# Gated feed-forwards of a 16-layer kernel: each fp32 product as three float32r products of operands split on chip

## Chip, cores, metric

One Trainium2 chip, one core. The metric is the device time of one execution in microseconds; the kernel before takes 3042.12 us (median of three runs, 3042.0 to 3043.24).

## What is computed

A stack of 16 layers on 1024 tokens of width 256, all in fp32: attentions, scans, and feed-forwards, each with a normalisation ahead of it and its result added to x. Six of them go through the function that is changed. With h the normalised tokens:

```python
# gated feed-forward (twice; 8 tiles of 128 inner rows; the gate has a low-rank part added)
out = (silu(h @ W_in.T + low_rank) * (h @ W_up.T)) @ W_down.T
# experts (twice; 32 experts x 96 inner rows = 24 tiles)
w = renormalised top-8 of softmax(h @ router.T), cut at a share of 0.8
out = sum_e w[:, e] * ((silu(h @ gate_e.T) * (h @ up_e.T)) @ down_e.T)
# ternary (twice; 704 inner rows, padded to 6 tiles; one scale per inner row and per output column)
out = (silu(h @ gate.T * gate_s) * (h @ up.T * up_s)) @ down.T * down_s
```

## The kernel before, in words

All layers run on one core, each in a stage of its own with five instruction streams (SP for transfers, TensorE, ScalarE, VectorE, GpSimd) that meet by semaphores. x and the transposed normalised tokens hT (128 x 2 x 1024) stay in SBUF. The end of a stage already makes the next one's first products and holds its first two weight tiles.

`gated_feed_forward` (L2227) does all six. A tile is 128 inner rows: 512 columns of gate and up weights and 256 of down weights, side by side in one of RING buffers (6, or 7 for the experts). A unit u is half a tile's tokens: tile u//2, tokens 512(u%2) onward. TensorE's order is written out by hand (L2413 to L2436): `project_gate(u)` (L2349), `project_up(u)` (L2373), then `lower(u - LAG)` (L2395), the down product of a unit LAG steps back (LAG 8, experts 10). Gate and up are two 128x512 matmuls each into PSUM; down is four matmuls of 256 columns, whose stationary side is a 128-token piece of the inner tile. ScalarE makes the silu (L2465), VectorE multiplies it by the up product into one of INNER buffers (L2484, ternary L2480). For the experts GpSimd then multiplies by the routing weight (L2338), which SP has spread over partitions (L2305) from a small DRAM table (L2313); for the ternary layers it scales the down weights in place (L2332). VectorE's routing chain (`choose`, L2493) has the first seven multiplies placed in it by hand, and TensorE transposes the routing weights in unit 7 (L2423). SP refills a weight buffer when the down product of its tile is done (L2296).

After the last unit the down products of the last LAG units are closed output tile by output tile (L2437 to L2446); each is added to x (L183), its statistics taken, its normalised row made and transposed for the next stage. Where the next layer has the kind "norm", VectorE has more steps for it (L237 to L243, L326). The core of TensorE's loop:

```python
for u in range(0, UNITS, 2):
    project_gate(u)
    if low_rank is None:
        project_up(u)
        if u >= LAG:
            lower(u - LAG)
        project_gate(u + 1)
```

Of the kernel before, what the change touches and what calls it, by code (L numbers as in the profile page):

```python
# [6 lines left out]
ALU = mybir.AluOpType  # L7
# [4 lines left out]
U32 = mybir.dt.uint32  # L12

P = 128
TOK = 1024
# [2211 lines left out]
def gated_feed_forward(core, name, first_w, tiles, source=None, scaled=False, low_rank=None, router=None,  # L2227
# [6 lines left out]

# [3 lines left out]
    UNITS, INNER, SPREAD = 2 * tiles, LAG + 2, 3  # L2238
# [5 lines left out]
    with Stage(core, name) as st:  # L2244
        following = core.next.open(st)
        block = st.opened
        w = [*first_w, *[st.sb(f"w{n}", [P, wide]) for n in range(len(first_w), RING)]]
        gate = [st.sb(f"gate{n}", [P, HALF]) for n in range(2)]
        inner = [st.sb(f"inner{n}", [P, HALF]) for n in range(INNER)]
        if router is not None:  # L2250
# [22 lines left out]
        copied, stored, found = st.sem("copied"), st.sem("stored"), st.sem("found")  # L2273

# [13 lines left out]
        def wait_inner(engine, u):  # L2288

            engine.wait_ge(multiplied if router is None else weighted, u + 1)  # L2290
# [54 lines left out]
        def _(pe):  # L2345
            def tokens_of(u):
                return slice(u % 2 * HALF, (u % 2 + 1) * HALF)

            def project_gate(u):  # L2349
                n = u // 2  # L2350
# [4 lines left out]
                wait_weights(pe, n)  # L2355
                if u >= 2:
                    pe.wait_ge(silued, u - 1)
                for c in range(DC):
                    last = nc.tensor.matmul(ps_gate[u % 2][:], w[n % RING][:, c * P:(c + 1) * P],  # L2359
                                            hT[:, c, tokens_of(u)], start=(c == 0),  # L2360
                                            stop=(c == DC - 1 and low_rank is None))
# [3 lines left out]
            def add_low_rank(u):  # L2365

                for half in range(2):
# [5 lines left out]
            def project_up(u):  # L2373
                n = u // 2
# [5 lines left out]
                for c in range(DC):  # L2380
                    last = nc.tensor.matmul(ps_up[u % 2][:], w[n % RING][:, D + c * P:D + (c + 1) * P],  # L2381
                                            hT[:, c, tokens_of(u)], start=(c == 0), stop=(c == DC - 1))
                last.then_inc(upped, 1)

            def down(u, t):
                return nc.tensor.matmul(out_of(t), inner[u % INNER][:, t % 4 * P:(t % 4 + 1) * P],  # L2386
                                        w[u // 2 % RING][:, 2 * D:3 * D], start=(u == 0), stop=(u >= UNITS - 2),
# [1504 lines left out]
```

## Time and profile before

| | |
|---|---|
| median of three runs | 3042.12 us |
| profiled execution: span, first to last instruction | 3038.4 us |
| its own time | not listed beside the runs; they are 3.6 to 4.8 us over its span |
| busy: TensorE, VectorE, ScalarE, GpSimd | 96%, 44%, 39%, 19% |
| mean granted TensorE clock | 0.993 |
| data moved | 121.96 MB, mean 40 GB/s |

Times in the profile are from the span's start. PE is TensorE's matmuls, PEld its loads of the stationary operand, DVE VectorE, ACT ScalarE, POOL GpSimd, SPq the transfer queue. An fp32 matmul appears as two records. A record's duration includes the pipeline, so neighbours overlap; the pitch is read from starts. In a timeline row that merges x records, the time is from the first's start to the last's end.

### The profile page before, as it was taken

The numbers are of one execution on the slowest core, as the hardware profiler recorded it, in microseconds if no ns is written. First come the engines' busy times: TensorE is split into PE (matmuls) and PEld (weight loads), VectorE is DVE, ScalarE is ACT, GpSimd is POOL, SyncE is SP. The second block draws the span as 40 slices with busy tenths as digits, with TensorE's granted clock in tenths as the row PEclk, the third lists the DMA queues.
The fourth block names the chain that finished last, engine by engine and source line by source line (L and its number), as shares of the span: only waits on it lengthen the run. The fifth ranks groups of instructions, "written<-read, shape, count | busy, mean of one in ns | idle before, by whom it ended". The sixth has DMA issues, their size and how long they took to land. (4 is left out here: it accounts for less than half of the span.)

```text
span 3038.4 us, 40714 instructions
## 1 busy us (share of the span) xinstructions
PE 2909.8 (96%) x14953; PEld 1767.2 (58%) x14953; DVE 1351.2 (44%) x3173; ACT 1171.7 (39%) x2389; POOL 586.7 (19%) x737
## 2 busy tenths in 40 slices
PE   7989999999999999999999999999999999999979
PEld 4444455644475555556666666646676677754545
DVE  7758425686144114211333333333333332258588
ACT  4636514546132113111443333433334343236576
POOL 2030001130012222222000000012333332130086
PEclk9999999999999999999999999999999999999999
DMA  3021000020102331332100000000000010121021
GB/s 98 18 67 47 26 25 27 9 79 2 51 12 87 88 99 50 90 92 85 39 16 11 11 11 11 18 32 11 12 16 11 16 39 13 39 43 43 13 88 60
DMA packets 69361, 121.96 MB, mean 40 GB/s; under 512 B 15790, under 2 KB 44816, under 8 KB 68896
## 3 DMA queue, kind: packets, MB, share of 16 engines
q1 hardware_dynamic: 67564, 118.04, 13.1%
q8 instruction: 121, 1.98, 0.3%
q10 hardware_dynamic: 1600, 1.31, 0.3%
q14 instruction: 76, 0.62, 0.1%
HBM read 92.21 MB, written 1.54 MB: 31 GB/s over the span
## 5 line engine op out<-in xcount | busy, mean ns | idle before, releaser
L222 POOL TENSOR_TENSOR scale<-scale,powers 128x1 f32<-128x1 f32 (+1 forms) x98 | 57.4, 586 | 1396.9 <-DVE scale L203 1396.9
L2484 DVE TENSOR_TENSOR L1f_inner<-psum,L1f_gate 128x512 f32<-128x512 f32 x96 | 66.4, 691 | 350.7 <-PE psum L2381 350.6
L1688 ACT ACTIVATE L2b_tanh<-psum,L2b_inverse 128x512 f32<-128x512 f32 x192 | 110.6, 579 | 269.7 <-PE psum L1636 268.3
L2465 ACT ACTIVATE L1f_gate<-psum 128x512 f32<-128x512 f32 x96 | 57.1, 597 | 388.0 <-PE psum L2359 388.0
L1267 ACT ACTIVATE L0f_weights<-psum 128x512 f32<-128x512 f32 (+2 forms) x320 | 156.9, 567 | 93.1 <-PE psum L1083 72.1
L2338 POOL TENSOR_TENSOR L1f_inner<-L1f_inner,L1f_weight 128x512 f32<-128x512 f32 x96 | 119.2, 1265 | 354.5 <-DMA L1f_weight<-combine 339.0
L1645 PEld LDWEIGHTS psum<-L2b_v,L2b_weights 128*128 128x128 f32 x1152 | 139.6, 191 | 40.2 <-issue 28.7
L2125 ACT ACTIVATE L2a_probs<-psum,L2a_negmax 128x512 f32<-128x512 f32 (+7 forms) x128 | 95.0, 742 | 172.4 <-DVE L2a_negmax L2159 172.3
L1636 PE MATMUL psum<-L2b_q,L2b_k 128*128 128x512 f32 (+3 forms) x384 | 149.9, 487 | 1.0 <-DVE L2b_q L1754 0.8
L1645 PE MATMUL psum<-L2b_v,L2b_weights 128*128 128x129 f32 x1152 | 143.6, 276 | 5.8 <-POOL L2b_weights L1554 5.8
L2012 PE MATMUL psum<-L2a_k,L2a_q 128*128 128x512 f32 (+3 forms) x384 | 145.1, 487 | 0.0
L2159 DVE TENSOR_REDUCE L2a_negmax<-psum 128x1 f32<-128x512 f32 (+7 forms) x128 | 96.6, 755 | 81.6 <-PE psum L2014 81.5
L2169 DVE COPY L2a_probsT<-psum 128x512 f32<-128x512 f32 (+1 forms) x64 | 31.4, 491 | 227.9 <-PE psum L2025 227.9
L2043 PE MATMUL psum<-L2a_probsT,L2a_v 128*128 128x512 f32 (+3 forms) x384 | 129.4, 486 | 0.3 <-DVEq L2197 0.3
L2386 PE MATMUL psum<-L1f_w,L1f_inner 128*128 128x256 f32 x512 | 122.9, 379 | 0.0
L1049 PE MATMUL psum<-L0f_ks,L0f_qs 96*128 96x512 bf16 (+3 forms) x384 | 111.3, 331 | 9.9 <-DVE L0f_piece_max L1348 5.6
L1995 PE MATMUL psum<-hT,L2a_early 128*128 128x512 f32 x248 | 119.8, 606 | 0.7 <-PEq L102 0.7
L2381 PE MATMUL psum<-hT,L1f_w 128*128 128x512 f32 x256 | 120.3, 592 | 0.0
L2359 PE MATMUL psum<-hT,L1f_w 128*128 128x512 f32 x256 | 120.3, 592 | 0.0
L1619 PE MATMUL psum<-hT,L2b_early 128*128 128x512 f32 x248 | 116.5, 593 | 1.0 <-PEq L102 1.0
L2386 PEld LDWEIGHTS psum<-L1f_w,L1f_inner 128*128 128x128 f32 x512 | 96.7, 190 | 35.0 <-issue 22.3
L1080 PE MATMUL psum<-L0f_qs,L0f_ks 99*128 99x512 bf16 (+3 forms) x384 | 111.8, 328 | 3.8 <-ACT L0f_weights L1267 2.1
(537 smaller groups left out, 6152.7 us busy)
## 6 DMA issues: line engine op xcount, KB each, us to landing
L1f_w<-in_L1f_w SPq DMA_DIRECT2D x32, 384.0 KB, 3.8
L1f_weight<-combine SPq DMA_DIRECT2D x32, 384.0 KB, 4.4
L1f_weight<-combine SPq DMA_DIRECT2D x32, 256.0 KB, 4.8
scan_spread_b<-bc SPq DMA_DIRECT2D x16, 512.0 KB, 3.8
L0f_qs<-L0f_part SPq DMA_DIRECT2D x96, 64.0 KB, 2.6
experts_early<-in_L1f_w SPq DMA_DIRECT2D x16, 384.0 KB, 3.4
L2a_early<-in_L2a_w SPq DMA_DIRECT2D x16, 384.0 KB, 3.0
L2b_early<-in_L2b_w SPq DMA_DIRECT2D x16, 384.0 KB, 3.1
```

What stands on the lines that cost most here:

```text
L1080: last = nc.tensor.matmul(to, ks[:, kt // 4, h, kt % 4 * P:(kt % 4 + 1) * P], qs[:, half, h, at:], start=True, stop=not masks)
L1267: nc.scalar.activation(to, src, ACT.Exp, scale=HD ** -0.5).then_inc(exped, 1)
L1619: last = nc.tensor.matmul(to[:], w[e][:, c, at:at + P], hT[:, c, half * HALF:(half + 1) * HALF], start=(c == 0), stop=(c == DC - 1))
L1636: nc.tensor.matmul(ps_scores[u % 3][:, at:], k[e][:, kt * P:(kt + 1) * P], q[e][:, half * HALF + at:(half + 1) * HALF], start=True, stop=T ...
L1645: last = nc.tensor.matmul(ps_out[t % 2][:, 0:P + 1], weights[UNITS.index((kt, t // 4))][:, at:at + P], v[e][:, kt, :], start=(kt == 0), st ...
L1995: last = nc.tensor.matmul(to[:], w[h % 2][:, c, at:at + P], hT[:, c, half * HALF:(half + 1) * HALF], start=(c == 0), stop=(c == DC - 1))
L2012: nc.tensor.matmul(ps_scores[i % 2][:, a:b], q[h % 2][:, t * P:(t + 1) * P], k[h % 2][:, a:b], start=True, stop=b < width(i))
L2043: last = nc.tensor.matmul(to[:, at:], v[h % 2][:, kt, :], probsT[h % 2][half][:, kt, at:], start=(kt == 0), stop=(kt == tiles - 1))
L2338: nc.gpsimd.tensor_tensor(inner[u % INNER][:], inner[u % INNER][:], weight[n % SPREAD][:, half * HALF:(half + 1) * HALF], ALU.mult).then_i ...
L2359: last = nc.tensor.matmul(ps_gate[u % 2][:], w[n % RING][:, c * P:(c + 1) * P], hT[:, c, tokens_of(u)], start=(c == 0), stop=(c == DC - 1 ...
L2381: last = nc.tensor.matmul(ps_up[u % 2][:], w[n % RING][:, D + c * P:D + (c + 1) * P], hT[:, c, tokens_of(u)], start=(c == 0), stop=(c == D ...
L2386: return nc.tensor.matmul(out_of(t), inner[u % INNER][:, t % 4 * P:(t % 4 + 1) * P], w[u // 2 % RING][:, 2 * D:3 * D], start=(u == 0), sto ...
```

## The change

Every operand of the three products is split on chip into a high part, a copy written as float32r, and its rest, the difference written as float32r. A product a.b becomes high.high + high.rest + rest.high, three matmuls into the same PSUM tile (`products`, `multiply_parts`). ScalarE makes the high parts, VectorE the rests. The gate and up products of the first WHOLE = 1 tile stay fp32; all down products are split. The tokens are split once per layer (four copies, four subtractions), the gate and up weights of a tile two tiles ahead, the down weights by `down_of_step`, the inner tile BEHIND steps after its multiply (1, experts 8). A weight buffer is now refilled when its down weights have been split. In the routing chain the token split and the steps' subtractions stand between the old steps. An excerpt of the diff:

```diff
+def products(stationary, moving):
+    return [(stationary[0], moving[0]), (stationary[0], moving[1]), (stationary[1], moving[0])]
+def multiply_parts(nc, to, pairs, start, stop, skip=False):
+    for n, (stationary, moving) in enumerate(pairs):
+        last = nc.tensor.matmul(to, stationary, moving, start=start and n == 0, stop=stop and n == len(pairs) - 1,
+                                skip_group_check=skip)
+    return last
...
-    UNITS, INNER, SPREAD = 2 * tiles, LAG + 2, 3
+    UNITS, WHOLE, WIDE_PARTS, DOWN_PARTS, SPREAD = 2 * tiles, 1, 3, LAG // 2 + 1, 3
+    BEHIND = 1 if router is None else LAG - 2
+    INNER = BEHIND + 2
...
+        def wide_of_step(s):
+            n = s // 2 + WHOLE + 1
+            return n if s % 2 == 0 and n < tiles else None
+        def down_of_step(s):
+            m = (s - LAG + 3) // 2
+            return m if s % 2 and 0 <= m < tiles else None
+        STEPS_IN_ALL = max(UNITS + BEHIND, 2 * tiles + LAG - 3)
...
-                    sp.wait_ge(lowered, 2 * (n - RING) + 2)
+                    sp.wait_ge(down_low, n - RING + 1)
...
+            def project(u, to, at, open_ended=False):
...
+                pe.wait_ge(hT_low, DC * 2)
+                pe.wait_ge(wide_low, n - WHOLE + 1)
+                pairs = []
+                for c in range(DC):
+                    pairs += products([part[:, at + c * P:at + (c + 1) * P] for part in wide_parts[n % WIDE_PARTS]],
+                                      [part[:, c, tokens_of(u)] for part in hT_parts])
+                return multiply_parts(nc, to, pairs, start=True, stop=not open_ended)
...
             def wait_down(u):
-                wait_inner(pe, u)
-                if down_by is not None:
-                    pe.wait_ge(down_scaled, u // 2 + 1)
+                pe.wait_ge(inner_low, u + 1)
+                pe.wait_ge(down_low, u // 2 + 1)
...
+            def high_wide(n):
+                wait_weights(act, n)
+                if n >= WHOLE + WIDE_PARTS:
+                    act.wait_ge(upped, 2 * (n - WIDE_PARTS) + 2)
+                nc.scalar.copy(wide_parts[n % WIDE_PARTS][0][:], w[n % RING][:, 0:2 * D]).then_inc(wide_high, 1)
...
+            def high_inner(u):
+                act.wait_ge(multiplied if router is None else weighted, u + 1)
+                if u >= LAG:
+                    act.wait_ge(lowered, u - LAG + 1)
+                nc.scalar.copy(inner_parts[u % LAG][0][:], inner[u % INNER][:]).then_inc(inner_high, 1)
...
+            for half in range(2):
+                for c in range(DC):
+                    high_tokens(c, half)
+            high_wide(WHOLE)
             if router is not None:
                 act.wait_ge(shifted, 1)
                 nc.scalar.activation(p[:], logits[:], ACT.Exp).then_inc(exped, 1)
-            for u in range(UNITS):
+            for s in range(STEPS_IN_ALL):
+                if s < UNITS:
+                    find_gate(s)
+                if wide_of_step(s) is not None:
+                    high_wide(wide_of_step(s))
+                if down_of_step(s) is not None:
+                    high_down(down_of_step(s))
+                if BEHIND <= s < UNITS + BEHIND:
+                    high_inner(s - BEHIND)
...
+            def low_inner(u):
+                dve.wait_ge(inner_high, u + 1)
+                high, low = inner_parts[u % LAG]
+                nc.vector.tensor_tensor(low[:], inner[u % INNER][:], high[:], ALU.subtract).then_inc(inner_low, 1)
...
                 nc.vector.tensor_tensor(logits[:], ps_logits, over_experts(peak), ALU.subtract).then_inc(shifted, 1)
+                low_tokens()
                 dve.wait_ge(exped, 1)
...
                 multiply(0)
+                after_multiply(0)
```

`high_down`, `low_wide`, `low_down` and `high_tokens` are of the same form; `low_tokens` ends with `low_wide(WHOLE)`, and `after_multiply(s)` makes VectorE's wide, down and inner rests of step s in that order.

## Rows read from the trace of the kernel before

**Rows 1.** The page's first part: busy time and share of the span by engine.
```profile
PE 2909.8 (96%) x14953; PEld 1767.2 (58%) x14953; DVE 1351.2 (44%) x3173; ACT 1171.7 (39%) x2389; POOL 586.7 (19%) x737
```

**Rows 2.** Timeline in mid-layer: start us, us, engine, line, operation, operands, count.
```profile
1102.49 1.88 PE L2359 MATMUL psum<-hT,L1f_w 128*128 128x512 f32 x4
...
1104.20 1.88 PE L2381 MATMUL psum<-hT,L1f_w 128*128 128x512 f32 x4
...
1105.92 1.89 PE L2386 MATMUL psum<-experts_early,L1f_inner 128*128 128x256 f32 x8
...
1107.65 1.88 PE L2359 MATMUL psum<-hT,L1f_w 128*128 128x512 f32 x4
```

**Rows 3.** Window of the first expert layer: stretch, length, busy by engine, clock, DMA.
```profile
922.45:1175.50 253.05, 253.00 (x821) 151.01 (x822) 58.99 (x147) 37.82 (x65) 65.81 (x63) 1.00 0.30 86
```

**Rows 4.** Groups by line and shape: busy us, mean ns of one, idle before.
```profile
L332 PE MATMUL psum<-zeros 128*128 128x512 bf16 x109 | 28.0, 393 | 0.0
...
L2025 PE MATMUL psum<-ident,L2a_probs 128*128 128x128 f32 x576 | 84.3, 273 | 6.7 <-ACT L2a_probsT L2133 4.9
...
L1645 PEld LDWEIGHTS psum<-L2b_v,L2b_weights 128*128 128x128 f32 x1152 | 139.6, 191 | 40.2 <-issue 28.7 <-POOL L2b_weights L1554 11.5
```

**Rows 5.** Timeline: bf16 matmuls; transposes; fp32 loads and matmuls of 129 columns.
```profile
1180.94 3.62 PE L332 MATMUL psum<-zeros 128*128 128x512 bf16 x16
...
1907.36 0.71 PE L2025 MATMUL psum<-ident,L2a_probs 128*128 128x128 f32 x5
...
2199.53 0.86 PEld L1645 LDWEIGHTS psum<-L2b_v,L2b_weights 128*128 128x128 f32 x7 [0.24 <-issue]
...
2199.75 0.83 PE L1645 MATMUL psum<-L2b_v,L2b_weights 128*128 128x129 f32 x6
```

**Rows 6.** Groups as in rows 4: ScalarE, VectorE and GpSimd.
```profile
L1695 ACT ACTIVATE L2b_weights<-L2b_tanh 128x512 f32<-128x512 f32 x96 | 59.5, 620 | 0.0
...
L1695 ACT ACTIVATE L2b_weights<-L2b_tanh 128x256 f32<-128x256 f32 x32 | 13.2, 413 | 0.0
...
L2484 DVE TENSOR_TENSOR L1f_inner<-psum,L1f_gate 128x512 f32<-128x512 f32 x96 | 66.4, 691 | 350.7 <-PE psum L2381 350.6
...
L3121 DVE TENSOR_TENSOR scan_fed<-scan_delta,hT 128x512 f32<-128x512 f32 x4 | 5.6, 1400 | 0.1
...
L2338 POOL TENSOR_TENSOR L1f_inner<-L1f_inner,L1f_weight 128x512 f32<-128x512 f32 x96 | 119.2, 1265 | 354.5 <-DMA L1f_weight<-combine 339.0 <-DVE L1f_inner L2484 15.5
```

**Rows 7.** Start of the first expert layer: one window, then the timeline.
```profile
926.26:945.70 19.44, 19.44 (x46) 8.51 (x46) 18.16 (x70) 5.56 (x9) 0.00 (x0) 1.00 0.14 57
...
948.55 1.04 PE L2423 MATMUL psum<-ident,L1f_weights 128*32 128x128 f32 x8
...
957.26 12.28 POOL L2338 TENSOR_TENSOR L1f_inner<-L1f_inner,L1f_weight 128x512 f32<-128x512 f32 x10 [38.99 <-DMA L1f_weight<-combine]
...
961.44 1.89 PE L2386 MATMUL psum<-experts_early,L1f_inner 128*128 128x256 f32 x8
```

**Rows 8.** Timeline, start of the first ternary layer.
```profile
2023.68 0.69 ACT L2465 ACTIVATE L2f_gate<-psum,L2f_early 128x512 f32<-128x512 f32 x1
...
2026.27 1.88 PE L2359 MATMUL psum<-hT,L2f_early 128*128 128x512 f32 x4
```

**Rows 9.** Timeline, end of the first expert layer.
```profile
1150.64 1.88 PE L2381 MATMUL psum<-hT,L1f_w 128*128 128x512 f32 x4
...
1156.45 0.42 DVE L183 TENSOR_TENSOR x<-x,psum 128x256 f32<-128x256 f32 x1 [3.14 <-PE psum L2386]
```

**Rows 10.** Timeline, end of the first gated layer, VectorE.
```profile
446.87 0.42 DVE L183 TENSOR_TENSOR x<-x,psum 128x256 f32<-128x256 f32 x1
...
448.82 0.42 DVE L183 TENSOR_TENSOR x<-x,psum 128x256 f32<-128x256 f32 x1 [0.20 <-PE psum L2386]
```

**Rows 11.** Windows behind that end, columns as in rows 3.
```profile
454.00:458.00 4.00, 0.84 (x5) 0.48 (x4) 3.69 (x17) 1.08 (x2) 1.96 (x4) 1.00 0.00 0
...
460.00:462.00 2.00, 2.00 (x5) 1.00 (x4) 0.59 (x3) 0.00 (x0) 0.00 (x0) 0.50 0.00 0
```

More of the change, by code:

```diff
@@ L12 @@
 U32 = mybir.dt.uint32
+F32R = mybir.dt.float32r
 P = 128
@@ L2247, in gated_feed_forward @@
         w = [*first_w, *[st.sb(f"w{n}", [P, wide]) for n in range(len(first_w), RING)]]
+        hT_parts = [st.sb(f"hT_part{i}", [P, DC, TOK], F32R) for i in range(2)]
+        wide_parts = [[st.sb(f"wide{n}_{i}", [P, 2 * D], F32R) for i in range(2)] for n in range(WIDE_PARTS)]
+        down_parts = [[st.sb(f"down{n}_{i}", [P, D], F32R) for i in range(2)] for n in range(DOWN_PARTS)]
         gate = [st.sb(f"gate{n}", [P, HALF]) for n in range(2)]
         inner = [st.sb(f"inner{n}", [P, HALF]) for n in range(INNER)]
+        inner_parts = [[st.sb(f"inner_part{n}_{i}", [P, HALF], F32R) for i in range(2)] for n in range(LAG)]
         if router is not None:
@@ L2354, in project_gate @@
                     return
-                wait_weights(pe, n)
                 if u >= 2:
                     pe.wait_ge(silued, u - 1)
[L2358 to L2361, printed above, removed]
+                last = project(u, ps_gate[u % 2][:], 0, open_ended=low_rank is not None)
                 if low_rank is None:
@@ L2379, in project_up @@
                     pe.wait_ge(multiplied, u - 1)
[L2380 to L2383, printed above, removed]
+                project(u, ps_up[u % 2][:], D).then_inc(upped, 1)
             def down(u, t):
-                return nc.tensor.matmul(out_of(t), inner[u % INNER][:, t % 4 * P:(t % 4 + 1) * P],
-                                        w[u // 2 % RING][:, 2 * D:3 * D], start=(u == 0), stop=(u >= UNITS - 2),
-                                        skip_group_check=True)
+                at = t % 4 * P
+                return multiply_parts(nc, out_of(t),
+                                      products([part[:, at:at + P] for part in inner_parts[u % LAG]],
+                                               [part[:] for part in down_parts[u // 2 % DOWN_PARTS]]),
+                                      start=u == 0, stop=u >= UNITS - 2, skip=True)
             def wait_down(u):
-                wait_inner(pe, u)
-                if down_by is not None:
-                    pe.wait_ge(down_scaled, u // 2 + 1)
+                pe.wait_ge(inner_low, u + 1)
+                pe.wait_ge(down_low, u // 2 + 1)
             def lower(u):
@@ L2456, in _, with find_gate @@
         def _(act):
-            if router is not None:
-                act.wait_ge(shifted, 1)
-                nc.scalar.activation(p[:], logits[:], ACT.Exp).then_inc(exped, 1)
-            for u in range(UNITS):
+            def find_gate(u):
                 act.wait_ge(gated, u + 1)
@@ L2527, in choose @@
                 multiply(2)
+                after_multiply(2)
                 for t in range(NT):
@@ L2542, in choose @@
                 multiply(5)
+                after_multiply(5)
                 multiply(6)
+                after_multiply(6)
                 for n in range(2):
@@ L2547, in choose, with low_tokens @@
                                           ).then_inc(copied, 1)
-            if router is not None:
+            def low_tokens():
+                for half in range(2):
+                    for c in range(DC):
+                        part = slice(half * HALF, (half + 1) * HALF)
+                        dve.wait_ge(hT_high, DC * half + c + 1)
+                        nc.vector.tensor_tensor(hT_parts[1][:, c, part], hT[:, c, part], hT_parts[0][:, c, part],
+                                                ALU.subtract).then_inc(hT_low, 1)
+                low_wide(WHOLE)
+            if router is None:
+                low_tokens()
+            else:
                 choose()
-            for u in range(0 if router is None else 7, UNITS):
-                multiply(u)
+            for s in range(0 if router is None else 7, STEPS_IN_ALL):
+                if s < UNITS:
+                    multiply(s)
+                after_multiply(s)
             for t in range(NT):
```

48 lines of the change are left out of this document (43 added, 5 removed).

## The prediction

> **What bounds the kernel now.** I read the page's first part first: TensorE is busy for 96% of the span, every other engine for less than half [rows 1]. Busy time of pipelined multiplies overstates work, so the next view is the timeline of one stretch in the middle of an expert feed-forward, where the starts of the groups give the true pitch. There the gate product starts at 1102.49, the up product at 1104.20, the down products at 1105.92 and the next unit's gate at 1107.65 [rows 2]. So a unit (half a tile: 128 inner rows x 512 tokens) costs 5.16 us: 3.43 for two products of two 128x512 fp32 matmuls each (0.86 us a matmul, two records of 0.43) and 1.72 for four 128x256 matmuls (0.43 each, two records of 0.215). TensorE starts each piece when the one before lets it go. The windows of a whole expert layer show the same: 253.00 of 253.05 us busy, VectorE 59, ScalarE 38, GpSimd 66, clock 1.00 [rows 3]. The bound is TensorE's column passes: four passes of a product's columns at 0.215 us per 512, in two records.
>
> The six gated layers have 16+16+48+48+12+12 = 152 units, so 152 x 5.16 = 784 us of the run is what the change touches.
>
> **What the change removes and adds on TensorE.** An fp32 matmul becomes three float32r ones. No row of this kernel runs that type. Lower bound of its price: the rate of a 2-byte operand, one column pass. The 16 bf16 128x512 matmuls, each with a load of its own, end 3.62 us after the first starts; less the last one's own 0.39 that is 15 pitches of 0.215 us [rows 4, 5]. Upper bound: one fp32 record, 0.43 us per 512 columns [rows 2]; the nearest row of a single 4-byte record, the transposes of 128 columns, speaks for it: 5 of them in 0.71 us, each 0.27 long, so (0.71 - 0.27)/4 = 0.11 us per 128 columns, twice the bf16 rate [rows 4, 5]. I take 0.215: an fp32 product here is exactly four passes of one column each, which is what two halves of one operand times two halves of the other would be, and a type made for operands cut to a high part has no reason to split again; the transposes move exact bits in 128-column pieces and need not be the same path. It stays the main uncertainty.
>
> The load of the stationary tile counts too, once per pass: in the down products a pass of 256 columns is only 0.107 us. The nearest rows are the 128x129 fp32 records with their loads: 7 loads of 0.19 in 0.86 us, (0.86 - 0.19)/6 = 0.112 us apart, beside 6 matmuls in 0.83, with the transposes' 0.27 for the last one (0.83 - 0.27)/5 = 0.11 apart [rows 4, 5]. A load per 0.112 us is hidden, so a down pass costs 0.111. The other bound is a load in the open at its full 0.19.
> - Gate and up: tile 0 stays fp32, so 140 units x 4 matmuls = 560, each 0.86 - 3 x 0.215 = 0.215 less: 120.4 us.
> - Down: all 152 units x 4 = 608, each 0.43 - 0.333 = 0.097 less: 59.0 us.
> - Sum 179.4 us. The unit becomes 2.58 + 1.33 = 3.91 us.
>
> A rule of the Trainium skill speaks against this. First the row: loads of 0.19 us follow each other at 0.112 us while matmuls on the same 128 rows run at 0.11 [rows 5], so they lie under them. The skill (TensorE: Matmul & The Clock Gate, What overlaps and what doesn't) says that a weight load overlaps running matmuls only when it goes to another row group; by that rule each of the new passes would show its load. The trace contradicts it, so I give it a small chance only; its price is a rival below.
>
> **The splitting work, beside TensorE.** Per unit ScalarE gets one 128x512 copy of the inner tile, and per tile one of 128x512 and one of 128x256. By its row of an SBUF source (620 and 413 ns) that is 0.62 + (0.62 + 0.41)/2 = 1.14 us on top of a 0.6 us silu. VectorE gets subtractions: 0.69 + (0.69 + 0.42)/2 = 1.25 us on top of its 0.69 multiply [rows 6, 10]. Both stay under 2 us in a 3.91 us unit. Each part is made ahead of use: wide parts four units, inner parts at least two, so these chains cost nothing while that lead holds. In the expert layers GpSimd's multiply (1.265 us a unit) reads the same memory; one 128x512 VectorE product of two SBUF tiles took 1.40 us where 0.69 is usual, which I read as such a clash [rows 6]. Even doubled, 2.5 + 0.69 = 3.2 us is below 3.91. Transfers: a weight tile's load now waits for the low part of the down weights, four units earlier than it waited for the down product; SP's queue is not longer and the order of the spread weights is unchanged. Cost 0.
>
> **The edges, where that lead does not exist.**
> - Start of an expert layer. VectorE runs the routing chain 18.16 us busy in the 19.44 up to 945.70, when the weights are reduced; TensorE asks for them only at 948.55, and the first down product starts at 961.44 [rows 7]. Now VectorE gets, inside that chain, four token subtractions and four to five wide ones (9 x 0.69 = 6.2, of which 0.5 fills a wait for ScalarE), so the routing weights come at 951.4; TensorE, now faster, waits for them. From the transposes to GpSimd's first product took 957.26 - 948.55 = 8.7 us (copies, a store, the spread) [rows 7]; with two multiplies and a subtraction now ahead of the copies 10.2, so GpSimd starts at 961.7. Its product, the copy, the subtraction (1.27 + 0.62 + 0.69) and handovers put the first down product at 964.6. Unhindered it would be at 961.44 - 9 x 0.86 = 953.7. Loss 10.9 us a layer, 22 in two.
> - Start of the other four. In a ternary layer silu used to start at 2023.68, behind its table load [rows 8]; it now stands behind five copies (3 us), and the gate product of unit 2, at 2026.27, waits for it: to 2027.4. Loss 1.2 each, 5 in all. The first layer's tokens are copied while the fp32 tile 0 runs, so that cover is nearly whole.
> - End of an expert layer. The low parts run 8 units behind the multiply, so after the last multiply VectorE still has 8 inner and 3 down subtractions and one more: about 8 us, with ScalarE beside it. Up to now four down matmuls were followed at once by the closing sums (last up product 1150.64, first sum 1156.45) [rows 9]. TensorE needs unit 46's part for its first closing sum and gets it 8 us after the last up product, having 2.9 us of work: loss 5.5 each, 11.
> - End of the other four: one unit behind, but three down parts late: 1.2 each, 5.
> - The first layer's end is followed by a norm with more VectorE steps: its sums already come 1.95 us apart (446.87, 448.82) against 1.72 of TensorE [rows 10], so the 8 x 0.4 us saved there is lost: 3.
> - Clock. After 3.2 us without work in 454 to 458 the granted clock was 0.50 in 460 to 462 [rows 11], which is the lower level. The new hole at the expert layers' ends may do it: 2.5 each, 5.
>
> Sum of the edges 51. Net 179 - 51 = **128 us less**. The rows are of one execution with a span of 3038.4 us; its own time is not listed, but the three runs (median 3042.12) are 3.7 us over the span, so I take that for what lies around it. 3042.1 - 128 = **2914 us**. Its own range: edges of 25 to 80 us and a down pass of 0.107 to 0.12 give 2885 to 2950.
>
> **Rivals.**
> - Slower: a float32r pass costs what one fp32 record costs. Place: every pass of the gated layers. Gate and up then cost 1.29 for 0.86 (+0.43 x 560 = +241), down 0.645 for 0.43 (+0.215 x 608 = +131); the edges half as much (+25): **3440 us**. For it: the transposes' 0.11 us. Against it: bf16's 0.215 [rows 5]. It decides from the pass price at which 560(0.86 - 3p) + 608(0.43 - 1.5p) = 51, p = 0.27 us per 512 columns. A compiler that turns these matmuls into the two-record form would be the same rival in a worse size. 0.11.
> - Loads in the open everywhere: 1680 + 1824 = 3504 passes x 0.111 = +389: **3303 us**. This is what the skill's rule would do here. Against it: the hidden loads [rows 5]. 0.03.
> - Only the down passes limited by loads of 0.19: 608 x (0.57 - 0.333) = +144: **3058 us**. 0.04, half of it so near no change that I count 0.02 there.
> - VectorE and GpSimd hold each other up in the expert layers, the unit going to 4.6 us rather than 3.91: 96 x 0.7 = +67: **2981 us**. For it: the doubled subtraction [rows 6]. 0.08.
> - The forecast: 0.74.
>
> **Numbers.** 0.2% (6 us) is about what a measurement of this kernel can tell from no change. Faster is forecast and the fourth rival: 0.82; same 0.02; slower 0.16. The range that holds 8 in 10 takes the forecast's own and the fourth rival: 2875 to 2990.
>
> **What would show it.** The new matmul records: single, 512 columns 0.215 us apart and 256 columns 0.107 to 0.112. A unit in mid-layer 3.9 us long, with no wait of TensorE for a low part. TensorE idle before the first down product of an expert layer and before its closing sums, nowhere else over 2 us. Passes 0.43 us apart, or a unit over 5.16 us, would prove the forecast wrong; so would VectorE busy without gaps in mid-layer.

## The result and the profile after

The changed kernel takes 2953.52 us (median of four runs, 2952.19 to 2954.47) beside 3042.06 us (four runs, 3040.25 to 3043.24) for the kernel before: a ratio of 0.9709, 95% interval 0.9695 to 0.9723. That is 88.5 us less, where the forecast was 128 less, so 39 us above the forecast. It lies inside the range given for 8 cases in 10 (2875 to 2990) and 3.5 us outside the forecast's own (2885 to 2950).

The first part of the profile's page, after:

```profile
span 2952.7 us, 44166 instructions
...
PE 2796.7 (95%) x16121; PEld 1871.8 (63%) x16121; DVE 1606.9 (54%) x3495; ACT 1324.7 (45%) x2711; POOL 613.0 (21%) x737
```

TensorE lost 113 us of busy time against [rows 1], VectorE gained 256 and ScalarE 153, and TensorE is still the bound. Groups by line (busy us, mean ns of one, then idle before):

```profile
L130 PE MATMUL psum<-L1f_hT_part,L1f_wide 128*128 128x512 f32 x1104 | 271.7, 396 | 6.1 <-DVE L1f_inner L2561 5.5
...
L2369 POOL TENSOR_TENSOR L1f_inner<-L1f_inner,L1f_weight 128x512 f32<-128x512 f32 x96 | 143.1, 1500 | 268.0 <-DVE L1f_inner L2561 177.6
L130 PE MATMUL psum<-L1f_down,L1f_inner_part 128*128 128x256 f32 x1152 | 159.7, 291 | 16.1 <-DVE L1f_inner_part L2577 16.1
...
L2577 DVE TENSOR_TENSOR L1f_inner_part<-L1f_inner,L1f_inner_part 128x512 fp32r<-128x512 f32 x96 | 142.3, 1491 | 10.5 <-ACT L1f_inner_part L2521 10.5
```

The float32r products are one record each (1104 is 92 units of two products of six; the labels say f32). TensorE has two new waits of some size: that for the inner tiles' rests, 16.1 us in 12 waits, and that for VectorE's multiply (L2561), 5.5 us in 9 waits, all of them at the layers' edges. Timeline of TensorE in mid-layer, to be held against [rows 2]:

```profile
1040.63 2.91 PE L130 MATMUL psum<-L1f_hT_part,L1f_wide 128*128 128x512 f32 x12
1043.37 1.59 PE L130 MATMUL psum<-L1f_down,L1f_inner_part 128*128 128x256 f32 x12
1044.81 2.91 PE L130 MATMUL psum<-L1f_hT_part,L1f_wide 128*128 128x512 f32 x12
```

Group starts give the pitch: 2.74 us for twelve gate and up passes, 1.44 for twelve down passes, no wait between them. The unit is 4.18 us; it was 5.16, and 3.91 was forecast. From start to start of single records a 512-column pass is 0.227 us and a 256-column pass 0.120.

Start of the first expert layer, TensorE (own products begin at 902.85), then its end:

```profile
902.85 5.38 PE L130 MATMUL psum<-hT,experts_early 128*128 128x512 f32 x8
...
926.86 1.03 PE L2461 MATMUL psum<-ident,L1f_weights 128*32 128x128 f32 x8
927.65 9.81 PE L130 MATMUL psum<-L1f_hT_part,L1f_wide 128*128 128x512 f32 x42
939.82 1.91 PE L130 MATMUL psum<-L1f_down,L1f_inner_part 128*128 128x256 f32 x12 [2.35 <-DVE L1f_inner_part L2577]
941.52 4.31 PE L130 MATMUL psum<-L1f_hT_part,L1f_wide 128*128 128x512 f32 x12
...
1097.71 1.95 PE L130 MATMUL psum<-L1f_down,L1f_inner_part 128*128 128x256 f32 x15
1101.34 0.63 PE L130 MATMUL psum<-L1f_down,L1f_inner_part 128*128 128x256 f32 x3 [1.68 <-DVE L1f_inner_part L2577]
1102.88 0.63 PE L130 MATMUL psum<-L1f_down,L1f_inner_part 128*128 128x256 f32 x3 [0.91 <-DVE L1f_inner_part L2577]
1104.42 0.62 PE L130 MATMUL psum<-L1f_down,L1f_inner_part 128*128 128x256 f32 x3 [0.91 <-DVE L1f_inner_part L2577]
1105.96 8.56 PE L130 MATMUL psum<-L1f_down,L1f_inner_part 128*128 128x256 f32 x48 [0.92 <-DVE L1f_inner_part L2577]
```

The hole ahead of the first down product and the one ahead of the closing sums are where the prediction put them, 2.35 and 4.4 us (1.68 + 0.91 + 0.91 + 0.92), and behind each TensorE runs slower. Windows (columns as in [rows 3], the last three numbers being clock, DMA share and GB/s):

```profile
940.00:945.00 5.00, 5.00 (x22) 4.23 (x23) 3.48 (x4) 0.45 (x1) 5.00 (x4) 0.66 0.59 184
1104.00:1112.00 8.00, 6.66 (x32) 6.46 (x33) 4.87 (x13) 0.60 (x1) 1.24 (x3) 0.57 0.01 2
```

A granted clock of 0.66 and 0.57 of 2.4 GHz means that most of each stretch ran at 1.2 GHz.

Where the time went, by stage (from a stage's first TensorE product to the next stage's first, one profiled execution each):

| stage | before | after | saved in passes at 0.227 and 0.120 | given back at the edges |
|---|---|---|---|---|
| gated, two layers | 100.6, 94.0 | 89.8, 81.2 | 14.6, 14.6 | 3.8, 1.8 |
| experts, two layers | 254.9, 255.0 | 228.3, 228.4 | 46.5, 46.5 | 19.9, 19.9 |
| ternary, two layers | 64.9, 64.3 | 56.7, 56.5 | 10.6, 10.6 | 2.4, 2.8 |
| all other stages, to TensorE's last product | 2201 | 2208 | 0 | 7 |

The fourth column: an fp32 product of 512 columns for three passes saves 0.86 - 0.68 = 0.18 us, one of 256 columns 0.43 - 0.36 = 0.07, so an expert layer saves 184 x 0.18 + 192 x 0.07 = 46.5. These prices are rounded. By the unit, which fell by 5.16 - 4.18 = 0.98 us where all of it is split and by 1.72 - 1.44 = 0.28 where only the down products are, an expert layer saves 46 x 0.98 + 2 x 0.28 = 45.6, and its edges give back 19.0.

### The profile page after: what moved, and what is told of

Read it like the earlier page. It is cut to its first block and busy times, and to the rows that moved or that the text cites. A ratio compares the mean times of both kernels' runs of the same rounds, so it can differ in the third digit from the quotient of the medians.

```text
span 2952.7 us, 44166 instructions
## 1 busy us (share of the span) xinstructions
PE 2796.7 (95%) x16121; PEld 1871.8 (63%) x16121; DVE 1606.9 (54%) x3495; ACT 1324.7 (45%) x2711; POOL 613.0 (21%) x737
## 3 DMA queue, kind: packets, MB, share of 16 engines
q10 hardware_dynamic: 1600, 1.31, 0.3%
## 5 line engine op out<-in xcount | busy, mean ns | idle before, releaser
L130 PE MATMUL psum<-L1f_hT_part,L1f_wide 128*128 128x512 f32 x1104 | 271.7, 396 | 6.1 <-DVE L1f_inner L2561 5.5
L130 PEld LDWEIGHTS psum<-L1f_hT_part,L1f_wide 128*128 128x128 f32 x1104 | 203.8, 190 | 50.8 <-DVE L1f_inner L2561 9.6
L2369 POOL TENSOR_TENSOR L1f_inner<-L1f_inner,L1f_weight 128x512 f32<-128x512 f32 x96 | 143.1, 1500 | 268.0 <-DVE L1f_inner L2561 177.6
L130 PE MATMUL psum<-L1f_down,L1f_inner_part 128*128 128x256 f32 x1152 | 159.7, 291 | 16.1 <-DVE L1f_inner_part L2577 16.1
L130 PEld LDWEIGHTS psum<-L1f_down,L1f_inner_part 128*128 128x128 f32 x1152 | 154.1, 198 | 25.0 <-DVE L1f_inner_part L2577 19.4
L2577 DVE TENSOR_TENSOR L1f_inner_part<-L1f_inner,L1f_inner_part 128x512 fp32r<-128x512 f32 x96 | 142.3, 1491 | 10.5 <-ACT L1f_inner_part L2521 10.5
L2147 ACT COPY L2a_probsT<-psum 128x512 f32<-128x512 f32 (+3 forms) x128 | 64.7, 505 | 124.1 <-PE psum L2039 122.3
L2561 DVE TENSOR_TENSOR L1f_inner<-psum,L1f_gate 128x512 f32<-128x512 f32 x96 | 66.0, 689 | 97.6 <-ACT L1f_gate L2500 94.0
```

The lines of the kernel that those rows point to most:

```text
L130: last = nc.tensor.matmul(to, stationary, moving, start=start and n == 0, stop=stop and n == len(pairs) - 1, skip_group_check=skip)
L2369: nc.gpsimd.tensor_tensor(inner[u % INNER][:], inner[u % INNER][:], weight[n % SPREAD][:, half * HALF:(half + 1) * HALF], ALU.mult).then_i ...
L2577: nc.vector.tensor_tensor(low[:], inner[u % INNER][:], high[:], ALU.subtract).then_inc(inner_low, 1)
```

## The experiments

The theory after the result: the mechanism is the one forecast (fewer column passes on TensorE, with the splitting hidden in mid-layer), and the miss is the price of a float32r pass, 12 and 9 ns over the forecast on each of 3504 passes. Rivals: the loads of the stationary tiles set the pitch; the edges or the split work cost more than they seem to. They come in the order of the argument.

**1. The price of a pass by itself.** In the changed kernel, a later stage first does 219 matmuls of no use to the result, in groups (2986.09 us in its single run):

```diff
+            group(r_wide, r_token, 20, 512)
+            group(r_wide, r_token, 20, 384)
...
+            group(r_wide, r_token, 20, 128)
+            group(r_wide, r_token, 19, 512, turn=True)
+            group(r_wide, r_token, 20, 480, m=32)
+            group(r_wide, r_token, 20, 240, m=32)
+            group(b_wide, b_token, 20, 512)
...
```

> One look. The decay stage gets extra matmuls whose results are dropped, on real data: float32r with a 128-column load of its own and 512, 384, 256, 192 and 128 columns, one group that changes its stationary tile each time, two groups that load only 32 columns (480 and 240 moving), and bf16 with 512, 256 and 128 columns. Theory A (a float32r pass has a fixed price of its own beside one column per 2.4 GHz cycle): pitches N/2.4 + 13 ns, so about 227, 173, 120, 93 ns, the same with a changing stationary tile, and still 213 and 113 ns with the 32-column load; bf16 without it: 215, 109. Theory B (the 13 ns are the 128-column 4-byte load that does not quite hide): with the 32-column load the pitch falls to 202 and 102 ns. At 128 columns the load may set the pitch (112 ns or more) under both.

Measured, the median time from one record's start to the next one's, in ns:

| columns | 512 | 384 | 256 | 192 | 128 | 480, 32 wide | 240, 32 wide |
|---|---|---|---|---|---|---|---|
| float32r | 227 | 173 | 120 | 111 | 111 | 213 | 107 |
| bf16 | 216 | | 109 | | 56 | | |

The weight loads of these groups (count, then the duration of one as min/median/max in ns, first and last start, forms):

```profile
L2833 PEld LDWEIGHTS psum<-decay_r_token,decay_r_wide x159: 107/188/193, 1135.7 to 1161.4; 128*128 128x128 f32 x119, 128*32 128x32 f32 x40
...
L2833 PEld LDWEIGHTS psum<-decay_b_token,decay_b_wide x60: 96/98/99, 1161.6 to 1169.1; 128*128 128x128 bf16 x60
```

At 2.4 GHz a column takes 0.417 ns, so 512, 384 and 256 columns are 213, 160 and 107 ns, and the pass is 13 ns more at each: a fixed part, not a rate. bf16 pays 2 to 3 ns. Below 256 columns another limit takes over: 111 ns, for 192 and for 128 columns alike, with a 4-byte 128x128 tile loaded before each, while a 2-byte tile allows 56. With a stationary tile of 32 columns, 240 moving columns go at 107, which is under that floor. So 111 is no floor of every 4-byte pass; it fits the 128-column load, and the down passes at 120 stay above it. Whether the 32-column load, itself 107 to 108 ns long, sets a floor at 107 was not run. The fixed 13 ns holds with one stationary address repeated and with two in turn (227 each). It does not hold at 240 columns with 32 wide, where 7 are left; that stays open. Nor does it hold at the lower clock: in the half-clock stretches of the changed kernel (942 to 945 and 1106 to 1111) the starts are 426 or 427 ns apart for 512 columns and 213 or 214 for 256, which is the columns at 1.2 GHz and nothing more.

The loads are 188 ns long and follow each other at 111 to 120 in the groups of 256 columns and fewer. So they lie under the matmuls on the same rows, as [rows 5] had said. The rule of the Trainium skill (TensorE: Matmul & The Clock Gate, What overlaps and what doesn't), that a load overlaps only matmuls of another row group, is not what these runs show.

**2. The parts in bfloat16.** This kernel rounds both parts to bfloat16, so the rest loses bits too and some 16 bits of each operand are kept, which is less than the change keeps (no run measured the error):

```diff
-        hT_parts = [st.sb(f"hT_part{i}", [P, DC, TOK], F32R) for i in range(2)]
+        hT_parts = [st.sb(f"hT_part{i}", [P, DC, TOK], BF16) for i in range(2)]
...
```

> All parts are stored as bf16 in place of float32r; everything else, the three passes, waits and order, stays. The rest is then rounded to 8 bits, so the third part of each operand's precision is left out. If the missing 39 us of the forecast are the float32r pass price (227 and 120 ns in place of 215 and 111), the passes go back to about 215 and 109 ns, 1680 x 0.012 + 1824 x 0.011 = 40 us less than the changed kernel: about 2914 us. If they come from the three-pass pattern, its loads or its waits, the time stays at about 2953.

2917.74 us (2917.41 to 2919.85), ratio 0.9597 (0.958 to 0.9613), 36 us less than the changed kernel. Mid-layer timeline of TensorE:

```profile
1043.21 2.75 PE L130 MATMUL psum<-L1f_hT_part,L1f_wide 128*128 128x512 bf16 x12
1045.80 1.47 PE L130 MATMUL psum<-L1f_down,L1f_inner_part 128*128 128x256 bf16 x12
1047.11 2.75 PE L130 MATMUL psum<-L1f_hT_part,L1f_wide 128*128 128x512 bf16 x12
```

The unit is 3.90 us, where 3.91 was forecast for float32r, and the time is 4 us from the forecast's 2914. Where the passes cost what the prediction had put for them (2.59 and 1.31 us for twelve), its sum comes out within 4 us; so the price was what was wrong.

**3 and 4. One half of the change at a time.** The down product back in fp32, with the old wait before a weight buffer's refill, and in another kernel gate and up back in fp32:

```diff
-                    sp.wait_ge(down_low, n - RING + 1)
+                    sp.wait_ge(lowered, 2 * (n - RING) + 2)
...
-                return multiply_parts(nc, out_of(t), ...
+                return nc.tensor.matmul(out_of(t), inner[u % INNER][:, at:at + P], w[u // 2 % RING][:, 2 * D:3 * D],
```

> Only gate and up products are split; the down products are fp32 again, with their old waits. By the pass price, 608 x (0.43 - 0.36) = 43 us are given back; the edges at the layers' ends (about 4.4 us of waits and some 3 us of half clock in each expert layer, 1.2 in the other four) go: 2953 + 43 - 20 = about 2976 us. The rival, that the down split hurts more than it brings because its edges and VectorE's extra work weigh more, says 2953 or less.

> Only the down products are split; gate and up are fp32 as before. By the pass price 560 x (0.86 - 0.68) = 101 us are given back, and the starts lose their waits (some 8 us in each expert layer, 1 to 2 in the others): 2953 + 101 - 22 = about 3032 us. With e3 this says whether the two savings add up: 43 + 101 of passes.

Down in fp32: 2998.4 us (2993.75 to 3005.49), ratio 0.9857 (0.9841 to 0.9874), 22 us over the expectation. Gate and up in fp32: 3025.6 us (3020.97 to 3026.68), 0.9947 (0.993 to 0.9963), within 7 us of it. The first shows a side of the change that the prediction had priced at nothing. ScalarE in mid-layer, timeline:

```profile
990.04 0.62 ACT L2505 CAST L1f_wide<-L1f_w 128x512 fp32r<-128x512 f32 x1 [7.46 <-DMA L1f_w<-in_L1f_w]
...
999.93 0.62 ACT L2505 CAST L1f_wide<-L1f_w 128x512 fp32r<-128x512 f32 x1 [8.29 <-DMA L1f_w<-in_L1f_w]
```

ScalarE waits for the weights themselves, and TensorE for the silu queued behind that copy (12.7 us in four waits in the gated layers, 7.5 in 19 in the expert layers). Gate and up weights are now needed two tiles ahead, but the buffer is refilled only once its down product is done. In the changed kernel the down weights are copied out early, so the refill starts early.

**5. The down product in fp32 with two more weight buffers** (the rings 8 and 9 instead of 6 and 7, else as the third):

```diff
-    LAG, RING = (8, 6) if router is None else (10, 7)
+    LAG, RING = (8, 8) if router is None else (10, 9)
```

> The second product in fp32 again, as in the run that took 2998.4 us, with two more weight buffers in the ring, so that a buffer's refill can start two expert pairs earlier. Theory A (what that run lost above its 2976 us was the refill, which goes back to waiting for the last product): 2972 to 2985 us, and the waits of ScalarE's weight rounding on the weight DMA go. Theory B (the fp32 product itself costs more than its share): 2993 to 3003 us.

2967.4 us (2965.94 to 2971.2), ratio 0.9763 (0.9748 to 0.9778): below both theories. ScalarE's waits for the weights are gone, and 31 us of the third kernel's loss were the late refill. What is left is that splitting the down product, 42.6 us of saved passes, is worth 14 us (2967.4 - 2953.4, the mean of the changed kernel's two medians). The stages say where. The four other layers take 294.9 us for 284.2, so there it pays 10.7. The expert layers take 228.4 and 229.3 us: practically what the changed kernel takes. Its timeline around the two edges:

```profile
934.61 9.81 PE L130 MATMUL psum<-L1f_hT_part,L1f_wide 128*128 128x512 f32 x42
944.45 1.99 PE L2424 MATMUL psum<-experts_early,L1f_inner 128*128 128x256 f32 x8
...
1106.68 3.08 PE L130 MATMUL psum<-L1f_hT_part,L1f_wide 128*128 128x512 f32 x12
1109.61 2.32 PE L2424 MATMUL psum<-experts_early,L1f_inner 128*128 128x256 f32 x10
1111.76 1.89 PE L2424 MATMUL psum<-L1f_w,L1f_inner 128*128 128x256 f32 x8
```

Neither hole is there and the clock stays at 1.00. Its 184 gate and up products save 33.1 us, so an expert layer gives back 228.4 - (254.9 - 33.1) = 6.6 us at its edges instead of 19.9. So 13.3 of the 19.9 come from the inner tiles' split, and that is what 192 down products save (13.4). In the expert layers half of the change earns nothing. (The changed kernel was not run with the larger ring; it has no wait for weights in mid-layer that the ring could remove.)

**6. Two passes instead of three.** This kernel leaves out rest.high, a third of the products' work:

```diff
-    return [(stationary[0], moving[0]), (stationary[0], moving[1]), (stationary[1], moving[0])]
+    return [(stationary[0], moving[0]), (stationary[0], moving[1])]
```

> The third product (rest times high) is left out, nothing else. TensorE's work falls by a third: 560 x 0.227 + 608 x 0.12 = 200 us, to a unit of 2.78 us, about 2755 us if the splitting stays hidden. If VectorE, which in the changed kernel needs 0.69 + 1.49 + 0.55 us a unit in the expert layers beside GpSimd's 1.5, is nearly the next bound there, the expert unit stays at 3.2 us or more and the time at 2790 or above. This measures how much cover is left.

2788.34 us (2787.04 to 2788.87), ratio 0.9168 (0.9154 to 0.9182). The run asks how near VectorE is to being the bound, and neither expectation came true as a whole. TensorE's waits for the inner tiles' rests grew from 16.1 to 26.9 us and those for VectorE's multiply from 5.5 to 13.8, all at the edges. Mid-layer timeline of TensorE:

```profile
1010.07 2.00 PE L130 MATMUL psum<-L1f_hT_part,L1f_wide 128*128 128x512 f32 x8
1011.91 1.12 PE L130 MATMUL psum<-L1f_down,L1f_inner_part 128*128 128x256 f32 x8
1012.86 2.00 PE L130 MATMUL psum<-L1f_hT_part,L1f_wide 128*128 128x512 f32 x8
```

The unit is 2.79 us, two thirds of 4.18, and mid-layer TensorE works without a wait. But a window of 80 us there has VectorE (the third number) without a gap too:

```profile
930.00:1010.00 80.00, 80.00 (x461) 70.45 (x460) 80.00 (x87) 43.64 (x86) 43.65 (x29) 1.00 0.59 167
```

At 2.79 us a unit the two engines tie, so the total comes out near what the theory of a VectorE bound had said, though through the edges: an expert layer has 48 units x 1.39 = 67 us of passes less and got 51 us shorter (228.3 to 177.3). The changed kernel at 4.18 us is well clear of that limit, and with VectorE's work as it is nothing below 2.8 us a unit could be had from TensorE alone (an inference from this tie, not a run).

**7 to 9. The edges.** The seventh kernel splits inner tiles three steps behind instead of eight once the routing is over, the eighth gives the token and first weight rests of the expert layers to GpSimd, which is idle there, and the ninth does both:

```diff
+        lag = BEHIND if router is None or s < 20 else 3
...
+                        nc.gpsimd.tensor_tensor(hT_parts[1][:, c, part], hT[:, c, part], hT_parts[0][:, c, part],
+                                                ALU.subtract).then_inc(hT_low, 1)
```

> In the expert layers the split of the inner tile, 8 steps behind the multiply, catches up from step 20 on by two tiles a step until it is 3 behind. Theory (the hole before the closing sums is VectorE's backlog): the 4.4 us of waits there shrink to 1 or 2 and the half clock behind it may go too: 3 to 6 us less a layer, 2941 to 2947 us. Rival (TensorE waits there for the last multiply and GpSimd's product in any case): no change, 2953.

> In the expert layers the rests of the tokens and of the first four split weight tiles are made by GpSimd, which is idle there, and leave VectorE's routing chain. Theory (the start is bound by that chain): the routing weights come some 5 us earlier, the first down product 4 to 5 us earlier, and the 2.35 us hole with its half clock may shrink: 8 to 12 us less in two layers, 2941 to 2945. Rival (GpSimd and VectorE hold each other up on shared memory access, and the spread of the routing weights sets the start): within 3 us of 2953.

> e6 and e7 together. If the two holes are separate, their gains add: 2930 to 2938 us.

2947.37 us (2945.3 to 2951.78; 0.9695, 0.9682 to 0.9708), 2950.27 (2947.73 to 2953.86; 0.9705, 0.9691 to 0.9718) and 2946.03 (2943.51 to 2947.35; 0.9689, 0.9675 to 0.9702). The intervals overlap that of the changed kernel, so a gain of 3 to 7 us is likely and none is certain. The seventh is 0.4 us over the upper end of its expectation, the eighth as the rival there had it, and the ninth missed. With the early split the end's hole is 2.7 us instead of 4.4:

```profile
1102.12 0.59 PE L130 MATMUL psum<-L1f_down,L1f_inner_part 128*128 128x256 f32 x3 [1.75 <-DVE L1f_down L2578]
1103.66 6.34 PE L130 MATMUL psum<-L1f_down,L1f_inner_part 128*128 128x256 f32 x51 [0.95 <-DVE L1f_down L2578]
```

In this execution of the seventh kernel those 51 passes run at full clock behind a hole of 2.7 us; at the end of the second expert layer, behind the same hole, some of them are at half clock.

The start has to be counted from each layer's own first TensorE product (896.49 with GpSimd's help, 899.28 without). With that help VectorE has eight subtractions less ahead of its sum of the routing weights, 4.8 us at a pitch of 0.6, yet that sum begins only 1.3 us sooner (23.9 for 25.2), and so do GpSimd's first weighted product (36.1 for 37.4) and the first down product (39.2 for 40.5). Both holes stay, 1.79 and 1.99 us for 2.35 and 1.28. GpSimd's timeline:

```profile
932.61 2.51 POOL L2380 TENSOR_TENSOR L1f_inner<-L1f_inner,L1f_weight 128x512 f32<-128x512 f32 x2 [17.00 <-DMA L1f_weight<-combine]
936.08 10.62 POOL L2380 TENSOR_TENSOR L1f_inner<-L1f_inner,L1f_weight 128x512 f32<-128x512 f32 x8 [0.96 <-DMA L1f_weight<-combine]
```

So what VectorE's chain gains is passed on in full, but it gains little. The trace says where the rest of the 4.8 us went. Three of VectorE's routing steps ran beside a GpSimd subtraction and took 0.94, 1.15 and 1.51 us for 0.42, 0.18 and 0.42, which is 2.6 us; 0.5 is a wait for ScalarE's exponential, and the chain's first step came 0.4 later. So the two engines do hold each other up, as the rival of this run had it. Behind the chain stands the path from the transposes over the spread of the weights to GpSimd's first product: 9.3 us here, 9.9 in the changed kernel, where 10.2 was forecast.

**10. The changed kernel once more**, to see what repeats:

> The changed kernel with no edit, beside the variants of this group. If the 7 us that the untouched layers lost and the granted clock of 0.984 belong to the change, they are there again: 2950 to 2956 us, untouched stages at 2208 us, clock 0.984. If they were an accident of one profiled execution, this profile shows untouched stages near 2201 us, at a clock above 0.986.

2953.25 us (2951.76 to 2958.27), ratio 0.9717 (0.9702 to 0.9731). The untouched stages took 2206 us at a mean clock of 0.987, between the two expectations. Over all the variants they took 2202 to 2210, against 2201 in the one profile of before. A part of the 7 us is one execution's: 2.8 of them lie in one attention stage (170.5 us before, 173.3 after), which took 170.3 in the repeat. How much belongs to the change stays open.

**11. Filling the hole.** 18 bf16 matmuls into a free PSUM tile before the closing sums of the expert layers:

```diff
+                pe.wait_ge(silued, UNITS - 1)
+                keep_busy(core, ps_gate[0], 18)
```

> The changed kernel with 18 bfloat16 matmuls of no use to the result set before the closing sums of each expert layer, where TensorE waits for the last inner tiles. Theory A (the hole lowers the granted clock, and the half-clock stretch behind it is what it costs): the stretch stays at full clock and each of the two expert layers gains about 3 us: 2945 to 2949 us. Theory B (the stretch has another cause, or the filling stands in the way of the sums as long as it saves): within 2 us of the changed kernel, 2951 to 2956 us.

2951.3 us (2946.53 to 2951.76), ratio 0.9699 (0.9686 to 0.9713). Timeline of TensorE, and two windows:

```profile
1100.27 3.83 PE L346 MATMUL psum<-zeros 128*128 128x512 bf16 x17
1103.75 2.18 PE L130 MATMUL psum<-L1f_down,L1f_inner_part 128*128 128x256 f32 x12
1106.86 6.02 PE L130 MATMUL psum<-L1f_down,L1f_inner_part 128*128 128x256 f32 x48 [0.92 <-DVE L1f_inner_part L2580]
```

```profile
1106.00:1110.00 4.00, 3.15 (x26) 3.15 (x27) 3.24 (x9) 0.16 (x1) 0.82 (x2) 1.00 0.02 4
1110.00:1114.00 4.00, 4.00 (x35) 4.00 (x35) 2.73 (x10) 1.91 (x4) 1.64 (x4) 1.00 0.00 0
```

The clock stays at 1.00 and 48 passes take 6.02 us instead of 8.56. The second expert layer's end is at full clock too, where the changed kernel had all four ends of two executions in part at half clock. So it was the hole that lowered the clock, and the end is 2.5 us shorter (1098.61 to 1112.72, against 1097.71 to 1114.36). Of that a layer keeps about 1, since the second hole at the layer's start was 3.04 us in this execution instead of 1.28. The longer hole itself costs nothing (the down product behind it starts 48.4 us after the layer's first own product, for 48.5), but the half-clock stretch behind it does: from there to the next down product it is 5.81 us for 4.28. The first layer took 227.2 us for 228.3. On the total, theory B's figure holds.

**12. Three edits together:** bfloat16 parts, the early split, a filling of 8. As in the second, less of each operand is kept.

> Three edits that were tried alone, together: the parts are bfloat16 instead of float32r (so the rest is rounded too and the products carry some 16 bits of each operand, which is less than the change keeps), the last inner tiles are split three steps sooner, and 8 bfloat16 matmuls fill the wait before the closing sums. If the gains add (2917.7 less 4 to 6 for the earlier split and up to 3 for the fill): 2908 to 2913 us, faster than both kernels. If the shorter passes make VectorE's split the bound at the layer's end, nothing is added: 2916 to 2920 us.

2910.56 us (2904.28 to 2914.13), ratio 0.9571 (0.9558 to 0.9584): inside its expectation and the lowest here among kernels that form all three part products, though at bfloat16's precision. Against the second kernel it is 7 us less, with intervals that overlap a little.

## Why the prediction was right, and where it was off

**What bounds the kernel: right.** TensorE's passes bound it before and after; a unit in mid-layer has no wait. The passes are single records, as said. That the time falls in the wide range is in part luck: the range was stretched to 2990 for the rival in which VectorE and GpSimd lengthen the unit, which did not come true. The forecast's own range was also added up too narrowly. Edges of 80 us and a down pass of 0.12 give 2959 and not 2950, and the other end is 2880.

**The price of a pass: the term that was mis-sized.** The step that took 0.215 us per 512 columns and 0.111 per 256 rested on the bf16 rows and on 129-column fp32 records [rows 4, 5]. A float32r pass costs 0.227 and 0.120. The sum of savings is 560 x 0.18 + 608 x 0.07 = 143.4 us, not 179.4 (141 by the unrounded units): 36 to 39 us less. The two profiled executions differ by 85.7 us, the medians by 88.5, so the profiles are 43 us short of the forecast's 128, and the untouched stages' 7 us are the rest. The error came from treating a pass as columns times a rate. With 3504 passes each 1 ns is 3.5 us, and the type's fixed part showed in no row of before. The range's own bound for a down pass, 0.107 to 0.12, did reach it; that for the wide pass had only its two ends, 0.215 and 0.43, and no value just above the lower one. The first run also gives the transposes' 0.11 us [rows 5] another reading than the one that spoke for the upper bound: 128 float32r columns go at 111 ns too, by the load and not by the columns, so that row could not tell the price of a column. The signs set beforehand, 0.107 to 0.112 for a down pass and 3.9 us for a unit, were both missed.

**Loads hidden: right**, 188 ns loads at a pitch of 111 to 120. They do set a floor, 111 ns, just below what the down passes need.

**Split work in mid-layer: right, for a reason worth seeing.** The inner tile's subtraction was counted at 0.69 us and at its double. It took 1.78, next to GpSimd's product, which rose from 1.265 [rows 6] to 1.5. VectorE's timeline in mid-layer, and the same instruction at the layer's end with GpSimd idle:

```profile
1040.06 0.41 DVE L2572 TENSOR_TENSOR L1f_down<-L1f_w,L1f_down 128x256 fp32r<-128x256 f32 x1
1040.39 1.78 DVE L2577 TENSOR_TENSOR L1f_inner_part<-L1f_inner,L1f_inner_part 128x512 fp32r<-128x512 f32 x1
...
1104.62 1.88 DVE L2577 TENSOR_TENSOR L1f_inner_part<-L1f_inner,L1f_inner_part 128x512 fp32r<-128x512 f32 x3
```

Three of them in 1.88 us when alone, one in 1.78 beside GpSimd. The fourth rival's mechanism was there and its price, an effect on the unit, was not: 90.87 us of VectorE in the 135 of 960 to 1095 leave a third free, and by the sixth kernel only a unit of 2.8 us would have used that up. The Trainium skill (SBUF — State Buffer, SBUF: two separate sides) calls the port pair of VectorE and GpSimd an exclusive lock: whichever starts first has it for its whole instruction, and the other blocks. The trace agrees on VectorE's side. Of the 96 subtractions of inner tiles, 70 took 1.76 to 1.78 us, and each of them began 0.17 to 0.52 us behind a GpSimd product. 24 took 0.68, with none under way when they began, six of these with one that began 0.16 to 0.39 later. The last two took 1.09, begun 0.73 behind one. A subtraction that began first:

```profile
1086.04 0.68 DVE L2577 TENSOR_TENSOR L1f_inner_part<-L1f_inner,L1f_inner_part 128x512 fp32r<-128x512 f32 x1
...
1086.20 1.67 POOL L2369 TENSOR_TENSOR L1f_inner<-L1f_inner,L1f_weight 128x512 f32<-128x512 f32 x1 [2.78 <-DVE L1f_inner L2561]
```

It does not agree on GpSimd's side: the products that began first mostly took 1.40 or 1.67 us, for 1.265 alone. No run took that apart.

**Transfers at cost 0: right in sum, wrong in kind.** The earlier refill is no neutral side of the change. Without it, 31 us are lost in the kernel with fp32 down products, as the third and fifth kernels show.

**The edges: right in sum, 50.6 us of 51.** An expert layer gave back 19.9 where 18.9 were said. At its start the first down product came 37.0 us after the first own product, where the sum had 38.5 and the kernel before 35.4; a second hole of 1.28 us and a half-clock stretch, which were not forecast there, made up the difference. 2.4 us of the start are waits for VectorE's multiplies inside the routing chain, which the prediction had not named. At its end 4.4 us of waiting for 5.5, and a half-clock stretch as forecast. The ternary layers gave back 2.4 and 2.8 for 2.4, the gated ones 3.8 and 1.8 for 5.4 and 2.4. That the sums agree to half a us is luck: by the unrounded units the edges are 48, and the terms miss by up to 1.6 us both ways. What the steps did not see is how this loss divides: two thirds of an expert layer's 20 us come from the inner tiles' split, so that in these layers the down product's part of the change was worth nothing.

**Clock.** The forecast of 2.5 us at each expert layer's end was right in size and place, as the filled hole shows. The mean granted clock fell from 0.993 to 0.984 and 0.987, with more short half-clock stretches all over the run. The 7 us in untouched stages were not in the sum and are only partly explained.

The slower rivals fell by the first measurement: a pass is 0.227 us, below the 0.27 from which the change would have cost time.

## What to carry to other kernels

Price a new matmul type per pass as a fixed part plus columns, and bound the fixed part on its own, since thousands of passes multiply it; measure one group of 20 first. Where a split adds a copy and a subtraction between a product and its use, mid-layer hides it and the layer's two ends pay it: compare what the part saves inside a layer with what it gives back there, layer kind by layer kind. A kernel that splits the inner tiles only in the four layers without routing would by these stages (an estimate) cost about nothing more and spare the expert layers' split work; it was not tried, and it needs the larger weight ring.

## What the runs showed of the hardware that was not expected

- A float32r pass has a fixed part of 13 ns over its columns at 2.4 GHz (227, 173 and 120 ns for 512, 384 and 256), bf16 one of 2 to 3 (216 and 109).
- With a 4-byte 128x128 stationary tile loaded before each, passes came 111 ns apart at the least, with a 2-byte one 56, while the records of the loads are 188 and 98 ns long.
- At half clock the fixed part is gone: 427 and 213 ns for 512 and 256 float32r columns.
- A subtraction of two SBUF tiles takes 0.68 us alone or when it starts 0.16 us ahead of a GpSimd product, and 1.78 when it starts 0.17 or 0.44 behind one; the product itself takes 1.5 on average for 1.265.
- Holes of 2.35 and 4.4 us in otherwise full work were followed by half-clock stretches. The length alone does not decide it: one of 2.23 us (tenth kernel) was followed by one, those of 2.13 and 2.32 us (eleventh and seventh) were not. With bf16 work of no use in the hole the clock stayed at 1.00.
